# Two layers of graph attention on one core: bracket's middle formed on VectorE, unit matrix of R added by GpSimd

## Chip, cores and metric
One core of a Trainium2 chip runs the whole program. The metric is the device time in microseconds (us). Engines: TensorE (PE; its weight loads are PEld), VectorE (DVE), ScalarE (ACT), GpSimd (POOL) and SyncE (SP), which issues the DMAs.

## What is computed
Layer 0 is a four-head graph attention over 4096 nodes; layer 1 is the one that the change touches. Cut to what matters:

```python
def top_p(Xa):                          # A: 4096 x 4096, row by row
    probs = softmax((Xa @ W1.T @ W2.T) @ (Xa @ W3.T).T)
    # keep the largest entries of a row until their sum reaches 0.9, drop the rest
    A = probs * mask
    return A / A.sum(-1)

R = adj + eye(N)                        # unit matrix on top of the adjacency
R = R / R.sum(-1)
Z = 0; Xf = Xa = X
for n in range(2):
    A = top_p(Xa)
    Xf = R @ Xf
    Xa = A @ Xa
    Z = Z + Xf @ U1[n].T + Xa @ U2[n].T
h = X + Z                               # then a layer norm, X added, a second layer norm
```

## The kernel before
Rows are handled in 32 tiles of 128. Layer 0 fills the first 1.6 ms. Layer 1 runs in two steps, `s` = 0 and 1. Step 1 (from 2.43 ms on) is where all of the change lies. Its engines each run their own program through the iterations n = 0, 1, ... of one software pipeline, and meet at semaphores only, so the order of an engine's instructions is that in which the code issues them:

- **TensorE** (`Tr`, `logits`, `zx`, `AV`, `mq`, `Rmul`): turns the masked row tile n-1, multiplies the logits of tile n+1, forms A @ Xa for tile n-1, a small product for tile n-2, and two row tiles of R @ Xf. The matrix R is never formed: `Rstart` (L690 to L697) puts the product of the identity with the tile's own rows of Xf into the PSUM bank, and `Rpart` adds 32 products with the adjacency's blocks, 257 columns wide; the last column of Xf is 1, so it collects the row sum of R.
- **ScalarE** (`expo`, `level`, `av_ev`, `mq_ev`, `r_ev`): softmax's exponential for tile n+1 (L971, then three small ones for the row's eight largest, `e8`), and for the same tile three levels of the top-p search (`level`, L979 to L1002). A level is two passes over 4096 columns (L988, L989) and five small operations that move the threshold; the first level starts with L987, which waits on semaphore `bt`, and its L995 waits on `bf`. `av_ev` (L1010) copies A @ Xa out of PSUM, `mq_ev` (L949, L952) two smaller results, `r_ev` (L1018) a row tile of R @ Xf.
- **VectorE** (`search`, `threshold`, `finish`): from ScalarE's threshold for tile n (semaphore `lt`, L1222) it makes levels 4 and 5 (L1226, each one pass over 4096 columns with two inputs from SBUF), then `rmax(n+1)` (L1173, L1174: the eight largest logits of the next tile, which lets ScalarE start `expo(n+1)`), then level 6 (L1226), `final_stats`, the pass L1232, and sixteen maxima, a sort of 48 candidates and some twenty small operations. It signals `lv`, marks entries (L1293, L1294), waits for GpSimd's all-reduce (L1334) and writes the masked tile (L1345).
- **GpSimd** (`r_post`, `bracket`, `scale_a`, `accumulate`, `final_second`, `final_first`, `levels`, `final_add`), in this order in an iteration: `r_post` scales two row tiles of R @ Xf by the reciprocal of their row sums; `bracket(n+1)` (L463 to L488) waits on `e8` and computes where the search starts: the middle `tst` = square root of (a6 * a4), signalled as `bt` after L475, then the factors of all levels, signalled as `bf` after L486; `scale_a` (L492 to L498) waits for `av_ev`, `accumulate` (L506) for `mq_ev`; `levels` (L460) is a maximum over partitions (`partition_all_reduce`).

Which iterations have the last layer norms is set by `fslot`: for n from 17 on, `final_add`, `final_first` and `final_second` (L525 to L541) stand on GpSimd between `accumulate` and `levels`, and four rows of `final_stats` (L1193 to L1196) on VectorE ahead of L1232. So the cycles up to 3536 us (called early ones here) and those from 3593 us (late ones) carry different work.

```python
b = rslot()
mm(b[:, 0:XA], ident_s, xf[:, r % NT, :], start=True, stop=False)      # L696
...
plink(tt(a(8), a(6), a(4), ALU.mult))                                   # L474
tt(tst[:, t % 2:t % 2 + 1], a(8), ahalf, ALU.pow).then_inc(g["bt"], 1)  # L475
```

`plink`, `link` and `alink` make the engine wait until its own instruction has finished. The functions that the change touches:

Of the kernel before, what the change touches and what calls it, by code (L numbers as in the profile page):

```python
# [9 lines left out]
ALU = mybir.AluOpType  # L10
# [5 lines left out]
TOP_P = 0.9  # L16
# [5 lines left out]
GEO = (0, 6)  # L22
ACT_LEVELS = 3
BISECT = 42


def gat_topp_kernel(nc, xT, x, adj, adjTb, Wp, WT, aT, res_w, bias, res_b, ident, sel,
                    W1, W2T, W3T, U1T, U2T, ln_g, ln_b, out):
    N = adj.shape[0]
    NT = N // 128  # L30
# [12 lines left out]
    AJR = 4  # L43
# [17 lines left out]
    with ctx:  # L61
# [208 lines left out]
        for s in range(2):  # L270
            g = {}
            for n in ("kt", "kc", "km", "kk", "pl", "el", "mx", "xp", "mask", "av", "R", "rv", "pz", "gx",
                      "gd", "po", "rd", "xs", "acc", "nz", "hi", "gi", "yd", "ys", "fi", "fa", "s1", "f1", "s2",
                      "fo", "fd", "lv", "lr", "lt", "qd", "e8", "bt", "bf", "xc"):
                g[n] = sem(f"{n}_{s}")
            g["aj"] = [sem(f"aj{i}_{s}") for i in range(AJR)]
            g["xd"] = [sem(f"xd{i}_{s}") for i in range(2)]
            st.append(g)
# [149 lines left out]
        def _(po):  # L428
# [26 lines left out]
            for s in range(2):  # L455
# [6 lines left out]
                def bracket(t):  # L462
                    a = lambda i: ptm[:, i:i + 1]  # L463
                    Z = zE[:, t % 2:t % 2 + 1]
                    po.wait_ge(g["e8"], t + 1)
                    h7, g7 = e8[:, 7:8], am[:, 8:9]
                    ts(a(0), Z, TOP_P, None, ALU.mult)
                    ts(a(1), h7, -1.0, 1.0, ALU.mult, ALU.add)  # L468
                    plink(ts(a(2), Z, (1 - TOP_P) / 4096 / 1.0001, None, ALU.mult))
                    ts(a(3), g7, a(0), None, ALU.is_ge)  # L470
                    plink(tt(a(5), h7, a(2), ALU.subtract))
                    ts(a(4), a(1), a(3), h7, ALU.mult, ALU.add)
                    plink(ts(a(6), a(5), a(3), a(2), ALU.mult, ALU.add))
                    plink(tt(a(8), a(6), a(4), ALU.mult))  # L474
                    tt(tst[:, t % 2:t % 2 + 1], a(8), ahalf, ALU.pow).then_inc(g["bt"], 1)  # L475
                    plink(tt(a(7), a(6), mone, ALU.pow))
                    plink(tt(a(9), a(7), a(4), ALU.mult))
                    f = fac[:, t % 2]
                    f2 = f.rearrange("p a b -> p (a b)")
                    plink(ts(f2, ones[:, 0:2 * LV], a(9), None, ALU.mult))  # L480
                    plink(tt(f2, f2, exps.rearrange("p a b -> p (a b)"), ALU.pow))
                    plink(ts(f[:, :, LV - 1], f[:, :, LV - 1], 1.0 + 2.0 ** -12, None, ALU.mult))
                    w = avg[:, t % 2]
                    tt(w[:, 0, :], f[:, 0, :], f[:, 1, :], ALU.add)
                    plink(tt(w[:, 1, :], f[:, 1, :], f[:, 0, :], ALU.subtract))
                    plink(ts(havg[:, t % 2].rearrange("p a b -> p (a b)"), w.rearrange("p a b -> p (a b)"),  # L486
                             0.5, None, ALU.mult))
                    po.sem_inc(g["bf"], 1)  # L488
# [19 lines left out]
                def r_post(p):  # L508
                    for i in range(2):
                        r = 2 * p + i  # L510
                        po.wait_ge(g["rd"], r + 1)
                        plink(tt(pq[:, 1, i:i + 1], prs[:, i, 256:257], mone, ALU.pow))
                        if p >= 1:
                            po.wait_ge(g["ys"], 32 * p)
                        o = ts(yr[:, i, :], prs[:, i, 0:256], pq[:, 1, i:i + 1], 0.0, ALU.mult, ALU.add)
                        if r < NT:
                            plink(o)
                            po.wait_ge(g["gi"], 32 * (p + 1))
                            o = tt(yr[:, i, :], yr[:, i, :], gxi[:, i, :], ALU.add)
                        o.then_inc(g["yd"], 1)  # L520
# [52 lines left out]
        def _(pe):  # L573
# [98 lines left out]
            for s in range(2):  # L672
# [17 lines left out]
                    return bank(6 + i % 2)  # L690

                def Rstart(r):
                    b = rslot()
                    if r >= NT:
                        pe.wait_ge(s_xl[r % NT // CT], 48)
                    mm(b[:, 0:XA], ident_s, xf[:, r % NT, :], start=True, stop=False)  # L696
                    return b  # L697

                def Rpart(r, b, lo, hi):
                    for j in range(lo, hi):  # L700
                        c, e = divmod(j, TBK)
                        q = r * NCH + c
                        if e == 0:
                            pe.wait_ge(g["aj"][q % AJR], 16 * (q // AJR + 1))
                        if r >= NT and j % CT == 0:
                            pe.wait_ge(s_xl[j // CT], 48)
                        last = mm(b[:, 0:XA], aj[:, q % AJR, e, :], xf[:, j, :], start=False, stop=(j == NT - 1))  # L707
                        if e == TBK - 1:
                            last.then_inc(g["R"], 1)

# [126 lines left out]
        def _(ac):  # L837
# [66 lines left out]
            for s in range(2):  # L904
# [119 lines left out]
                for t in range(2):  # L1024
                    zx_ev(None, t)
                    mq_ev(None, t)
                    if s == 0:
                        gx_ev(t)
                def acts(t, items):
                    items = list(items)  # L1030
                    for k in range(1, ACT_LEVELS + 1):
                        if t < NT:
                            level(t, k)
                        if k >= ACT_LEVELS - 1 and items:
                            r_ev(items.pop(0))
                    for r in items:
                        r_ev(r)
# [5 lines left out]
                for n in range(NT + 2):  # L1043
# [13 lines left out]
                        zx_ev(tz, tx)  # L1057
                    if n + 1 < NT:
                        expo(n + 1)
                    if 1 <= n <= NT:  # L1060
                        av_ev(n - 1)
                    if zm:
                        mq_ev(tz, tx)
                    if s == 0 and tx is not None:
                        gx_ev(tx)
                    if s == 1:
                        acts(n + 1, [2 * p + i for p in pairs_in(n) for i in range(2)])
                barrier(ac, kS[s])

        @block.vector  # L1070
        def _(ve):
# [94 lines left out]
            for s in range(2):  # L1166
# [32 lines left out]
                def final_stats(n):  # L1199
# [4 lines left out]
                    if s == 1 and n - 1 in fslot:  # L1204
                        for r in (2 * fslot[n - 1], 2 * fslot[n - 1] + 1):
                            ve.wait_ge(g["fa"], r + 1)
                            stats_of(r, g["s1"])

                def search(t):
                    E = eb[:, t % 2, 0:N]  # L1210
                    VN = V[:, 0:N]
# [2 lines left out]
                    if r:  # L1214
                        ve.wait_ge(g["xp"], t + 1)
                        link(v.tensor_scalar(theta, Z, TOP_P, None, ALU.mult))
                        if t == 0:
                            ve.wait_ge(g["bf"], 1)
                            link(v.tensor_copy(mid, tst[:, 0:1]))
                        else:  # L1220
# [2 lines left out]
                        for k in range(ACT_LEVELS + 1 if t else 1, r + 1):  # L1223
                            if k == r and t + 1 < NT:
# [3 lines left out]
                            link(v.tensor_scalar(tmp, G, theta, avg[:, t % 2, 1, k - 1:k], ALU.is_lt, ALU.mult))  # L1228
                            link(v.scalar_tensor_tensor(out=mid, in0=tmp, scalar=fac[:, t % 2, 0, k - 1:k], in1=mid,
                                                        op0=ALU.add, op1=ALU.mult))  # L1230
                        final_stats(t)
                        link(v.scalar_tensor_tensor(out=VN, in0=E, scalar=mid, in1=E, op0=ALU.is_le,  # L1232
                                                    op1=ALU.mult, accum_out=G))
                        link(v.tensor_tensor(ghi, Z, G, ALU.subtract))
# [176 lines left out]
```

## Time and profile before
| | |
|---|---|
| Median of 3 runs | 4351.58 us (4349.74 to 4353.28) |
| Profiled execution: its time | 4350.77 us |
| Profiled execution: span from the first instruction to the last | 4349.0 us |
| PE busy | 3762.5 us, 87% |
| DVE busy | 3623.6 us, 83% |
| ACT busy | 3114.5 us, 72% |
| POOL busy | 1017.3 us, 23% |
| Mean granted TensorE clock | 0.942 |

The busy shares are means over the whole program. No engine is near 100%, so within a stage the order in which engines wait for each other counts: the chain of waits follows the work that ended last back from one instruction to what released it, and the timeline shows what each engine did meanwhile. Times in both count from the start of the span.

### The profile page before, as it was taken

The page shows a single profiled execution, that of the slowest core. Times are in us where ns is not written, and L with a number is a line of the kernel's source. Part 1 is how long each engine was busy: PE and PEld are TensorE (multiplying, and loading weights), DVE is VectorE, ACT ScalarE, POOL GpSimd, SP SyncE. Part 2 cuts the span into 40 slices and gives each one's busy share as a digit, 9 for nine tenths or more (in the row PEclk, how much of TensorE's full clock was granted, in tenths as well). Part 3 has the DMA queues.
Part 4 walks back from the last instruction along what each step waited for, and adds up shares of the span by engine and source line. Part 5 has one row for each costly group of instructions (what it writes and reads, how often), then busy time and mean ns, then how long its engine had stood idle before and what let it go on. Part 6 is the DMA issues. An engine that isn't in the chain of part 4 may idle for free.

```text
span 4349.0 us, 66313 instructions
## 1 busy us (share of the span) xinstructions
PE 3762.5 (87%) x25364; PEld 3163.1 (73%) x25364; DVE 3623.6 (83%) x6400; ACT 3114.5 (72%) x3128; POOL 1017.3 (23%) x1412
## 2 busy tenths in 40 slices
PE   8677877777777769999999749999999999999996
PEld 5677777777777747777778547777777777778875
DVE  2899999999999939888888188888888889999995
ACT  3789889898989845555555367777777777777771
POOL 0000000000000000001010224444444445555555
PEclk9899999999999989999999979999999999999998
DMA  3211111111111020000000212222233423333332
GB/s 116 93 45 66 45 55 56 47 64 47 64 47 64 27 78 12 19 16 19 16 17 17 87 35 85 87 83 88 88 93 93 134 90 105 107 107 105 100 104 73
DMA packets 131759, 292.49 MB, mean 67 GB/s; under 512 B 14122, under 2 KB 94186, under 8 KB 127058
## 3 DMA queue, kind: packets, MB, share of 16 engines
q1 hardware_dynamic: 131410, 287.99, 20.6%
q8 instruction: 201, 3.29, 0.3%
q14 instruction: 148, 1.21, 0.1%
HBM read 250.19 MB, written 37.75 MB: 66 GB/s over the span
## 4 chain that ended last, share of the span: by engine, by line
PE 34%; ACT 28%; DVE 14%; issue 14%; POOL 10%; DMA 1%; DVEq 0%; SPq 0%; ACTq 0%; POOLq 0%
PE ps L803 11%; PE ps L642 9%; DVE b L1226 7%; ACT b L871 6%; ACT b L988 5%; ACT b L989 5%; DVE b L1173 3%; ACT b L865 3%; PE ps L792 3%; ACT b L971 3%; PE ps L748 3%; PE ps L623 2%; POOL b L468 2%; ACT b L859 1%; PE ps L780 1%
## 5 line engine op out<-in xcount | busy, mean ns | idle before, releaser
L707 PE MATMUL ps<-b 128*128 128x257 f32 x4096 | 902.1, 379 | 0.0
L803 PE MATMUL ps<-b 128*128 128x257 f32 x4096 | 900.9, 379 | 0.0
L642 PE MATMUL ps<-cb,b 128*128 128x128 f32 x4096 | 606.9, 312 | 321.7 <-ACT b L865 321.7
L707 PEld LDWEIGHTS ps<-b 128*128 128x128 f32 x4096 | 775.6, 189 | 118.3 <-issue 3.8
L803 PEld LDWEIGHTS ps<-b 128*128 128x128 f32 x4096 | 770.2, 189 | 111.7
L642 PEld LDWEIGHTS ps<-cb,b 128*128 128x128 f32 x4096 | 546.1, 163 | 371.1 <-ACT b L865 329.6
L1137 DVE SCALAR_TENSOR_TENSOR b<-b 128x4096 f32<-128x4096 f32 x128 | 566.4, 4425 | 63.1 <-ACT b L859 59.8
L1139 DVE CUSTOM_DVE_ANT_0 b<-b 128x4096 f32<-128x4096 f32 x128 | 566.3, 4425 | 5.5 <-DMA b<-in_adj 1.1
L871 ACT ACTIVATE b<-ps 128x1024 f32<-128x1024 f32 x512 | 499.9, 1023 | 75.6 <-PE ps L642 74.0
L623 PE MATMUL ps<-b 128*64 128x128 f32 x8192 | 504.0, 276 | 0.0
L865 ACT ACTIVATE b<-b 128x4096 f32<-128x4096 f32 x128 | 474.4, 3706 | 8.0 <-DVE b L1141 8.0
L623 PEld LDWEIGHTS ps<-b 128*64 128x64 f32 x8192 | 442.5, 137 | 43.1 <-issue 39.7
L1226 DVE SCALAR_TENSOR_TENSOR b<-b 128x4096 f32<-128x4096 f32 x99 | 453.0, 4576 | 2.6 <-DVE b L1222 0.2
L792 PE MATMUL ps<-cb,b 128*128 128x128 f32 x2048 | 265.5, 291 | 172.4 <-DVE b L1345 115.0
L792 PEld LDWEIGHTS ps<-cb,b 128*128 128x128 f32 x2048 | 250.6, 151 | 201.0 <-DVE b L1345 121.7
L436 POOL TENSOR_TENSOR cb<-cb 128x1 f32<-128x1 f32 x32 | 39.4, 1231 | 1518.6 <-DVE cb L1123 1518.6
L971 ACT ACTIVATE b<-b 128x4096 f32<-128x4096 f32 x64 | 237.0, 3704 | 197.9 <-DVE b L1174 197.9
L988 ACT ACTIVATE b<-b 128x4096 bf16<-128x4096 f32 x93 | 345.0, 3709 | 7.7 <-ACT b L1018 5.7
L989 ACT ACTIVATE b<-b 128x4096 bf16<-128x4096 f32 x93 | 345.0, 3709 | 3.0
L1345 DVE SCALAR_TENSOR_TENSOR b<-b 128x4096 f32<-128x4096 f32 x64 | 287.0, 4484 | 67.2 <-issue 41.7
L859 ACT ACTIVATE b<-b 128x2560 f32<-128x2560 f32 x128 | 310.9, 2430 | 2.3 <-SPq L216 2.3
L1051 ACT ACTIVATE b<-ps 128x1024 f32<-128x1024 f32 x256 | 244.5, 1029 | 59.8 <-PE ps L792 55.2
(186 smaller groups left out, 4743.2 us busy)
## 6 DMA issues: line engine op xcount, KB each, us to landing
b<-in_adjTb SPq DMA_DIRECT2D x256, 512.0 KB, 3.8
b<-in_adj SPq DMA_DIRECT2D x32, 2048.0 KB, 8.0
y_d<-b SPq DMA_DIRECT2D x64, 128.0 KB, 1.7
h_d<-b SPq DMA_DIRECT2D x64, 128.0 KB, 1.8
b<-h_d SPq DMA_DIRECT2D x64, 128.0 KB, 2.3
b<-in_xT SPq DMA_DIRECT2D x1, 4096.0 KB, 15.8
b<-in_x SPq DMA_DIRECT2D x32, 128.0 KB, 2.2
b<-y_d SPq DMA_DIRECT2D x32, 128.0 KB, 2.1
```

The source lines that it names most:

```text
L623: last = mm(bank(6 + t % 2)[half, 128 * h:128 * h + 128], h_s[:, j, 64 * h:64 * h + 64], pt[:, gq % PTR, b, :], start=(j < 2), stop=(j >= ...
L642: last = nc.tensor.transpose(bank(2 * (gq % 3), 2)[:, b * 128:(b + 1) * 128], ub[:, u % UB, j * 128:(j + 1) * 128], ident_s)
L707: last = mm(b[:, 0:XA], aj[:, q % AJR, e, :], xf[:, j, :], start=False, stop=(j == NT - 1))
L792: last = nc.tensor.transpose(o[:, b * 128:(b + 1) * 128], eb[:, t % 2, j * 128:(j + 1) * 128], ident_s)
L803: last = mm(o[:, 0:XA], at[:, q % ATR, b, :], xa[:, j, :], start=(j == 0), stop=(j == NT - 1))
L865: act(b, b, ACT.Exp, bias=nm[:, u:u + 1], accum_out=zp[:, u:u + 1]).then_inc(s_x, 1)
L871: act(pt[:, gq % PTR].rearrange("p a b -> p (a b)"), bank(2 * (gq % 3), 2)[:, 0:CW], ACT.Copy).then_inc(s_ev, 1)
L988: alink(act(junk, e, ACT.Sign, bias=neg, accum_out=C))
L989: alink(act(junk, e, ACT.Relu, bias=neg, accum_out=S))
L1137: link(v.scalar_tensor_tensor(out=b, in0=b, scalar=SLOPE, in1=b, op0=ALU.mult, op1=ALU.max))
L1139: link(v.tensor_tensor_reduce(out=b, in0=b, in1=adj_s[:, t % 2, :], scale=1.0, scalar=-3.0e38, op0=ALU.mult, op1=ALU.max, accum_out=nm[:, ...
L1226: link(v.scalar_tensor_tensor(out=VN, in0=E, scalar=mid, in1=E, op0=ALU.is_gt, op1=ALU.mult, accum_out=G))
```

## The change
Three things are changed, all in step 1.

1. **The bracket's middle.** VectorE forms the product under the root in three small operations (`bracket_head`), between its level 6 and `final_stats`, and signals `bh`. GpSimd's `bracket` waits for that instead of `e8` and takes the root as its first operation; the product a8 is gone, the rest of `bracket` follows. VectorE's pass over the tile (L1232 before, L1249 now) waits for the root (`bt`).
2. **ScalarE's order.** `av_ev` and `mq_ev` stood between `expo` and the first level. In step 1 they now stand behind the first level.
3. **The unit matrix of R.** `Rstart` issues no product any more, the first adjacency block starts the sum, and `r_post` on GpSimd adds the tile's rows of Xf (257 columns, the ones among them) ahead of the reciprocal.

```diff
--- before.py
+++ after.py
@@ -22,6 +22,7 @@
 GEO = (0, 6)
 ACT_LEVELS = 3
 BISECT = 42
+LEAST = (1 - TOP_P) / 4096 / 1.0001
 
 
 def gat_topp_kernel(nc, xT, x, adj, adjTb, Wp, WT, aT, res_w, bias, res_b, ident, sel,
@@ -271,7 +272,7 @@
             g = {}
             for n in ("kt", "kc", "km", "kk", "pl", "el", "mx", "xp", "mask", "av", "R", "rv", "pz", "gx",
                       "gd", "po", "rd", "xs", "acc", "nz", "hi", "gi", "yd", "ys", "fi", "fa", "s1", "f1", "s2",
-                      "fo", "fd", "lv", "lr", "lt", "qd", "e8", "bt", "bf", "xc"):
+                      "fo", "fd", "lv", "lr", "lt", "qd", "e8", "bt", "bf", "xc", "bh"):
                 g[n] = sem(f"{n}_{s}")
             g["aj"] = [sem(f"aj{i}_{s}") for i in range(AJR)]
             g["xd"] = [sem(f"xd{i}_{s}") for i in range(2)]
@@ -462,17 +463,17 @@
                 def bracket(t):
                     a = lambda i: ptm[:, i:i + 1]
                     Z = zE[:, t % 2:t % 2 + 1]
-                    po.wait_ge(g["e8"], t + 1)
+                    po.wait_ge(g["bh"], t + 1)
+                    m = tst[:, t % 2:t % 2 + 1]
+                    tt(m, m, ahalf, ALU.pow).then_inc(g["bt"], 1)
                     h7, g7 = e8[:, 7:8], am[:, 8:9]
                     ts(a(0), Z, TOP_P, None, ALU.mult)
                     ts(a(1), h7, -1.0, 1.0, ALU.mult, ALU.add)
-                    plink(ts(a(2), Z, (1 - TOP_P) / 4096 / 1.0001, None, ALU.mult))
+                    plink(ts(a(2), Z, LEAST, None, ALU.mult))
                     ts(a(3), g7, a(0), None, ALU.is_ge)
                     plink(tt(a(5), h7, a(2), ALU.subtract))
                     ts(a(4), a(1), a(3), h7, ALU.mult, ALU.add)
                     plink(ts(a(6), a(5), a(3), a(2), ALU.mult, ALU.add))
-                    plink(tt(a(8), a(6), a(4), ALU.mult))
-                    tt(tst[:, t % 2:t % 2 + 1], a(8), ahalf, ALU.pow).then_inc(g["bt"], 1)
                     plink(tt(a(7), a(6), mone, ALU.pow))
                     plink(tt(a(9), a(7), a(4), ALU.mult))
                     f = fac[:, t % 2]
@@ -509,6 +510,7 @@
                     for i in range(2):
                         r = 2 * p + i
                         po.wait_ge(g["rd"], r + 1)
+                        plink(tt(prs[:, i, :], prs[:, i, :], xf[:, r % NT, :], ALU.add))
                         plink(tt(pq[:, 1, i:i + 1], prs[:, i, 256:257], mone, ALU.pow))
                         if p >= 1:
                             po.wait_ge(g["ys"], 32 * p)
@@ -690,11 +692,7 @@
                     return bank(6 + i % 2)
 
                 def Rstart(r):
-                    b = rslot()
-                    if r >= NT:
-                        pe.wait_ge(s_xl[r % NT // CT], 48)
-                    mm(b[:, 0:XA], ident_s, xf[:, r % NT, :], start=True, stop=False)
-                    return b
+                    return rslot()
 
                 def Rpart(r, b, lo, hi):
                     for j in range(lo, hi):
@@ -704,7 +702,7 @@
                             pe.wait_ge(g["aj"][q % AJR], 16 * (q // AJR + 1))
                         if r >= NT and j % CT == 0:
                             pe.wait_ge(s_xl[j // CT], 48)
-                        last = mm(b[:, 0:XA], aj[:, q % AJR, e, :], xf[:, j, :], start=False, stop=(j == NT - 1))
+                        last = mm(b[:, 0:XA], aj[:, q % AJR, e, :], xf[:, j, :], start=(j == 0), stop=(j == NT - 1))
                         if e == TBK - 1:
                             last.then_inc(g["R"], 1)
 
@@ -1026,11 +1024,16 @@
                     mq_ev(None, t)
                     if s == 0:
                         gx_ev(t)
-                def acts(t, items):
+                def acts(t, items, n):
                     items = list(items)
                     for k in range(1, ACT_LEVELS + 1):
                         if t < NT:
                             level(t, k)
+                        if k == 1:
+                            if 1 <= n <= NT:
+                                av_ev(n - 1)
+                            if n >= 2 or n + 2 < NT:
+                                mq_ev(n - 2 if n >= 2 else None, n + 2 if n + 2 < NT else None)
                         if k >= ACT_LEVELS - 1 and items:
                             r_ev(items.pop(0))
                     for r in items:
@@ -1057,14 +1060,15 @@
                         zx_ev(tz, tx)
                     if n + 1 < NT:
                         expo(n + 1)
-                    if 1 <= n <= NT:
-                        av_ev(n - 1)
-                    if zm:
-                        mq_ev(tz, tx)
-                    if s == 0 and tx is not None:
-                        gx_ev(tx)
-                    if s == 1:
-                        acts(n + 1, [2 * p + i for p in pairs_in(n) for i in range(2)])
+                    if s == 0:
+                        if 1 <= n <= NT:
+                            av_ev(n - 1)
+                        if zm:
+                            mq_ev(tz, tx)
+                        if tx is not None:
+                            gx_ev(tx)
+                    else:
+                        acts(n + 1, [2 * p + i for p in pairs_in(n) for i in range(2)], n)
                 barrier(ac, kS[s])
 
         @block.vector
@@ -1206,6 +1210,14 @@
                             ve.wait_ge(g["fa"], r + 1)
                             stats_of(r, g["s1"])
 
+                def bracket_head(t):
+                    Z = zE[:, t % 2:t % 2 + 1]
+                    ve.wait_ge(g["e8"], t + 1)
+                    link(v.scalar_tensor_tensor(out=x_, in0=Z, scalar=TOP_P, in1=am[:, 8:9], op0=ALU.mult,
+                                                op1=ALU.is_le))
+                    link(v.scalar_tensor_tensor(out=x_, in0=Z, scalar=LEAST, in1=x_, op0=ALU.mult, op1=ALU.max))
+                    v.tensor_scalar(tst[:, t % 2:t % 2 + 1], x_, e8[:, 7:8], None, ALU.mult).then_inc(g["bh"], 1)
+
                 def search(t):
                     E = eb[:, t % 2, 0:N]
                     VN = V[:, 0:N]
@@ -1215,6 +1227,7 @@
                         ve.wait_ge(g["xp"], t + 1)
                         link(v.tensor_scalar(theta, Z, TOP_P, None, ALU.mult))
                         if t == 0:
+                            bracket_head(0)
                             ve.wait_ge(g["bf"], 1)
                             link(v.tensor_copy(mid, tst[:, 0:1]))
                         else:
@@ -1228,7 +1241,11 @@
                             link(v.tensor_scalar(tmp, G, theta, avg[:, t % 2, 1, k - 1:k], ALU.is_lt, ALU.mult))
                             link(v.scalar_tensor_tensor(out=mid, in0=tmp, scalar=fac[:, t % 2, 0, k - 1:k], in1=mid,
                                                         op0=ALU.add, op1=ALU.mult))
+                        if t + 1 < NT:
+                            bracket_head(t + 1)
                         final_stats(t)
+                        if t + 1 < NT:
+                            ve.wait_ge(g["bt"], t + 2)
                         link(v.scalar_tensor_tensor(out=VN, in0=E, scalar=mid, in1=E, op0=ALU.is_le,
                                                     op1=ALU.mult, accum_out=G))
                         link(v.tensor_tensor(ghi, Z, G, ALU.subtract))
```

The lines of the changed file stand two or more lower or higher than those of the kernel before; the instructions below say which is which. A row gives line, operation, output and inputs (b is the pool of SBUF, ps is PSUM, cb the constants), its width, and the semaphores it waits for.

GpSimd, a late iteration, from the second row tile of `r_post` on, before:

```order
L512 TENSOR_TENSOR b<-b,cb 128x1 [waits rd_1]
L515 TENSOR_SCALAR b<-b 128x256 [waits ys_1,s_pc]
L467 TENSOR_SCALAR b<-b 128x1 [waits e8_1]
L468 TENSOR_SCALAR b<-b 128x1
L469 TENSOR_SCALAR b<-b 128x1
L470 TENSOR_SCALAR b<-b 128x1 [waits s_pc]
L471 TENSOR_TENSOR b<-b 128x1
L472 TENSOR_SCALAR b<-b 128x1 [waits s_pc]
L473 TENSOR_SCALAR b<-b 128x1
L474 TENSOR_TENSOR b<-b 128x1 [waits s_pc]
L475 TENSOR_TENSOR b<-b,cb 128x1 [waits s_pc]
L476 TENSOR_TENSOR b<-b,cb 128x1
```

and now:

```order
L513 TENSOR_TENSOR b<-b 128x257 [waits rd_1]
L514 TENSOR_TENSOR b<-b,cb 128x1 [waits s_pc]
L517 TENSOR_SCALAR b<-b 128x256 [waits ys_1,s_pc]
L468 TENSOR_TENSOR b<-b,cb 128x1 [waits bh_1]
L470 TENSOR_SCALAR b<-b 128x1
L471 TENSOR_SCALAR b<-b 128x1
L472 TENSOR_SCALAR b<-b 128x1
L473 TENSOR_SCALAR b<-b 128x1 [waits s_pc]
L474 TENSOR_TENSOR b<-b 128x1
L475 TENSOR_SCALAR b<-b 128x1 [waits s_pc]
L476 TENSOR_SCALAR b<-b 128x1
L477 TENSOR_TENSOR b<-b,cb 128x1 [waits s_pc]
```

The root (L475 before, L468 now) has moved from the ninth place of `bracket` to the first; the product L474 is gone; each row tile of `r_post` has one instruction more, L513.

VectorE, a late iteration, from `rmax`'s last instruction on, as it is now:

```order
L1178 TENSOR_SCALAR b<-b 128x1 [waits s_dv]
L1239 SCALAR_TENSOR_TENSOR b<-b 128x4096
L1241 TENSOR_SCALAR b<-b 128x1 [waits s_dv]
L1242 SCALAR_TENSOR_TENSOR b<-b 128x1 [waits s_dv]
L1216 SCALAR_TENSOR_TENSOR b<-b 128x1 [waits e8_1,s_dv]
L1218 SCALAR_TENSOR_TENSOR b<-b 128x1 [waits s_dv]
L1219 TENSOR_SCALAR b<-b 128x1 [waits s_dv]
L1197 BN_STATS b<-b 128x6 [waits f1_1]
```

The three instructions L1216, L1218 and L1219 are new; L1197 is the first of `final_stats`, and at the end of `final_stats` stands the pass that now waits for `bt_1` as well:

```order
L1199 TENSOR_SCALAR b<-b 128x1 [waits s_dv]
L1200 TENSOR_SCALAR b<-b 128x1
L1249 SCALAR_TENSOR_TENSOR b<-b 128x4096 [waits s_dv,bt_1]
L1251 TENSOR_TENSOR b<-b 128x1 [waits s_dv]
L1255 MAX b<-b 128x8 [waits s_dv]
L1255 MAX b<-b 128x8 x15
```

ScalarE, the first of the three levels and what stands around it, before:

```order
L1010 ACTIVATE b<-ps 128x257 [waits s_ac,xs_1,av_1]
L949 ACTIVATE b<-ps 128x256 [waits s_ac,acc_1,pl_1]
L952 ACTIVATE kr<-ps 128x128 [waits s_ac]
L987 ACTIVATE b<-b 128x1 [waits s_ac,bt_1]
L988 ACTIVATE b<-b 128x4096 [waits s_ac]
L989 ACTIVATE b<-b 128x4096 [waits s_ac]
L990 ACTIVATE b<-b 128x1 [waits s_ac]
L991 ACTIVATE b<-b 128x1 [waits s_ac]
L992 ACTIVATE b<-b 128x1 [waits s_ac]
L995 ACTIVATE b<-b 128x1 [waits bf_1,s_ac]
L997 ACTIVATE b<-b 128x1 [waits s_ac]
```

and now:

```order
L985 ACTIVATE b<-b 128x1 [waits s_ac,bt_1]
L986 ACTIVATE b<-b 128x4096 [waits s_ac]
L987 ACTIVATE b<-b 128x4096 [waits s_ac]
L988 ACTIVATE b<-b 128x1 [waits s_ac]
L989 ACTIVATE b<-b 128x1 [waits s_ac]
L990 ACTIVATE b<-b 128x1 [waits s_ac]
L993 ACTIVATE b<-b 128x1 [waits bf_1,s_ac]
L995 ACTIVATE b<-b 128x1 [waits s_ac]
L1008 ACTIVATE b<-ps 128x257 [waits xs_1,av_1,s_ac]
L947 ACTIVATE b<-ps 128x256 [waits s_ac,acc_1,pl_1]
L950 ACTIVATE kr<-ps 128x128 [waits s_ac]
L986 ACTIVATE b<-b 128x4096 [waits s_ac]
```

L1010, L949 and L952 (now L1008, L947 and L950) have moved behind L997 (now L995).

## Rows read from the trace of the kernel before
**Rows 1.** Source view of line L1174 (VectorE), 2518 to 3537 and 3592 to 4209 us.
```profile
L1174 DVE TENSOR_SCALAR b<-b x19: 153/154/155, 2518.6 to 3536.3; 128x1 f32<-128x1 f32 x19
L1174 DVE TENSOR_SCALAR b<-b x12: 153/154/155, 3593.1 to 4208.0; 128x1 f32<-128x1 f32 x12
```

**Rows 2.** Chain of waits, 3196 to 3239 us: start us, us, what.
```profile
3196.69 0.16 DVE b L1174
...
3201.75 0.26 POOL b L467
3202.07 4.31 POOL b L468
...
3207.95 0.20 POOL b L474
3208.23 0.58 POOL b L475
3208.83 0.21 ACT b L987
...
3238.23 0.16 DVE b L1222
```

**Rows 3.** Timeline, same cycle: start us, us, engine, line, operation, shapes.
```profile
3201.84 4.48 DVE L1232 SCALAR_TENSOR_TENSOR b<-b 128x4096 f32<-128x4096 f32 x1
...
3213.31 0.25 POOL L486 TENSOR_SCALAR b<-b 128x12 f32<-128x12 f32 x1
...
3204.08 0.39 ACT L1010 ACTIVATE b<-ps 128x257 f32<-128x257 f32 x1 [2.47 <-PE ps L803]
...
3217.81 0.39 ACT L995 ACTIVATE b<-b 128x1 f32<-128x1 f32 x1
```

**Rows 4.** Chain of waits, 3759 to 3815 us, one later cycle.
```profile
3759.60 0.17 DVE b L1174
...
3774.48 0.23 POOL b L492
...
3786.63 0.73 POOL b L541
...
3793.14 0.40 POOL b L460
...
3799.25 0.17 DVE b L1222
...
3814.56 0.16 DVE b L1174
```

**Rows 5.** Timeline of VectorE and GpSimd, same later cycle.
```profile
3764.50 0.22 DVE L1229 SCALAR_TENSOR_TENSOR b<-b 128x1 f32<-128x1 f32 x1
3764.76 0.43 DVE L1193 BATCH_NORM_STATS2 b<-b 128x6 f32<-128x256 f32 x1
...
3768.91 4.49 DVE L1232 SCALAR_TENSOR_TENSOR b<-b 128x4096 f32<-128x4096 f32 x1
...
3768.90 2.31 POOL L481 TENSOR_TENSOR b<-b 128x12 f32<-128x12 f32 x1
3771.30 2.19 POOL L482 TENSOR_SCALAR b<-b 128x2 f32<-128x2 f32 x1
```

**Rows 6.** Timeline of VectorE and GpSimd in the cycle at 3870 us.
```profile
3878.94 4.49 DVE L1232 SCALAR_TENSOR_TENSOR b<-b 128x4096 f32<-128x4096 f32 x1
...
3879.14 6.45 POOL L481 TENSOR_TENSOR b<-b 128x12 f32<-128x12 f32 x1
...
3886.91 0.23 POOL L492 TENSOR_SCALAR b<-b 128x1 f32<-128x1 f32 x1 [0.19 <-POOL b L486]
```

**Rows 7.** Waits of TensorE, 2520 to 3536 and 3593 to 4208 us: total, times, longest.
```profile
PE ps L792 <- ACT b L1051: 57.0, 18, 4.7
PE ps L792 <- DVE b L1345: 35.1, 11, 4.4
```

**Rows 8.** Groups of instructions: the product with the identity.
```profile
L696 PE MATMUL ps<-b,cb 128*128 128x257 f32 x128 | 38.9, 386 | 3.7 <-SPq L216 3.7
```

## The prediction
> **What bounds the kernel now.** The page comes first: no engine is near 100%, so the sum is not to be made from busy times. All edits lie in step 1, and there one instruction per row tile marks the cycle: L1174, with which VectorE releases ScalarE's exponential. The source view gives its first and last start [rows 1]: 18 early cycles from 2518.6 to 3536.3 us, 56.54 us each, and 11 late ones from 3593.1 to 4208.0, 55.9 each. The chain of waits then says what closes a cycle; below, times count from L1174's start.
>
> An early cycle [rows 2]: exponential and e8 until 5.06, where GpSimd's bracket begins; its root is out and ScalarE's L987 starts at 12.14; three levels; VectorE takes over at 41.54 (L1222) and the rest of the cycle, 15.0, goes to levels 4 and 5 and `rmax`. VectorE, idle before L1222, and TensorE, which waits in every cycle for ScalarE's copies (57.0 us in 18 waits [rows 7]), are not the bound. The striking row is L468: 4.31 us for one column. It started just after L1232 (at 5.15, 4.48 us long [rows 3]) and came out when that pass ended.
>
> A late cycle closes elsewhere [rows 4]: not the levels on ScalarE but GpSimd's queue. scale_a starts at 14.88, the layer norms end at 27.76, the all-reduce starts at 33.54 (5.8 us in which the page shows nothing, since GpSimd changes its configuration for it), then VectorE writes the tile and reaches L1222 at 39.65. Here whatever makes GpSimd late makes the cycle late.
>
> **The change, early cycles.** Before, L1229 of level 6 is followed by L1193 0.26 us later [rows 5]; in the early cycles level 6 ends at 5.15, where L1232 starts [rows 3]. Three linked operations at 0.27 each: the third starts at 5.70 and ends near 5.9. GpSimd needs about a tenth to start, 0.58 for the root (L475 [rows 2]): ScalarE starts at 6.6, not 12.14. Gross gain 5.5.
>
> Two things take it back. First, the rest of bracket. VectorE's pass waits for the root, so it starts at 6.6 too, not 5.15, and again one of GpSimd's next operations gets stuck behind it. L468 came free 4.54 after the pass's start [rows 2, 3], and from there to the end of L486 it was 7.18 [rows 2, 3]; without the product (0.28, L474 to L475) and the root (0.58) 6.32 remain. The factors come at 6.6 + 4.54 + 6.32 = 17.5, 0.6 later than before (16.87). ScalarE's L995 reads them 8.98 after L987's start [rows 2, 3], so it would be there at 15.6; with 0.14 for the signal it gets them at 17.65, a new wait of 2.1. Second, the PSUM copies: they lay in the wait for the root and cost nothing (L1010 at 7.39, 0.39 long [rows 3]); that cover is gone, and three instructions of 0.4 or less with the gaps between them are 1.5 on the path (1.1 if there were no gaps, 2 if each ended a wait of its own). From L995 to L1222 it was 20.42 [rows 2, 3], now 21.9: L1222 at 39.6, and with 15.0 a cycle of 54.6. Saved: 2.0 x 18 = 35 us.
>
> **Late cycles.** VectorE's third operation is out at 5.9, the four row statistics take 4.15 (3764.76 to 3768.91 [rows 5]), so the pass starts at 9.97, not 9.31. The root is long there, no wait. On GpSimd L481, which raises the factors to their powers, starts at 9.30 today [rows 5], 4.24 after bracket's first operation; without product and root that is 3.38, behind the new root, which ends at 6.56: 9.94. So again it starts just ahead of the pass, as now (3768.90 against 3768.91 [rows 5]), runs its 2.31 beside it, and the next one (L482) is stuck until the pass ends. The factors came at 14.7, just ahead of L492, and come at 15.35, in time for ScalarE at 15.6. But scale_a, which waited only for bracket to end (14.88), now waits for av_ev, behind the first level: 6.6 + 8.98 to L995, 0.7 for it and L997, 0.4 for the copy, 0.15 for the signal = 16.85. **GpSimd's whole queue moves 1.97 us later,** the all-reduce and L1222 with it, since VectorE waits for that all-reduce in each late cycle. ScalarE's own levels would be done at 6.6 + 29.4 [rows 2] + 1.5 = 37.5, so what they gain ends in a wait. Twelve such cycles (the last one, from 4208.0 on, too) cost 23.6.
>
> One late cycle is already disturbed: at 3870 us L481 started 0.20 after the pass and took 6.45 [rows 6]. ScalarE's e8 had come late there; now VectorE waits for e8 as well, so both shift alike and some 2.4 come back. Late cycles net: +21.
>
> **Edits with one answer.** The cycle at 3536 us, with two of the four statistics, loses what it gains within 0.3. The first bracket, for which VectorE has nothing else to do, gets 0.5 longer. The products with the identity take at most 38.9 us in all [rows 8], on an engine that waits anyway [rows 7]: 0. The bound below is a gain of that size. The two additions on GpSimd per iteration, 257 columns, are priced by L541 at 0.73 [rows 4]. In the worst case they push the bracket by 1.5 a cycle, 45 us in all; but between the second row tile and the next bracket GpSimd has nothing to do: 0. In an early cycle the all-reduce starts 2 us later, VectorE's wait for it has that much room because its pass is 1.5 later too: 0.
>
> Sum against the profiled execution: 4350.8 - 35 + 21 + 1 = **4338 us**. The median shown, 4351.6, stands 0.8 above; I leave the forecast at 4338.
>
> **A rule against the trace.** L481 runs beside the whole first half of L1232, and that pass keeps its 4.49 [rows 5]. The Trainium skill, page "SBUF — State Buffer", section "Who interferes with whom", says that a VectorE instruction with two SBUF inputs contends with a GpSimd one that reads SBUF, and that whichever issued first has the shared ports for its whole instruction. The second half of that does not hold for this power operation; that the later one is fully blocked agrees with L468's 4.31 and L481's 6.45. By the row the sum stays at 4338; by the rule L481, starting clearly ahead, would hold the pass back, and the time would be the last rival's 4365.
>
> **Rivals.**
> - **L481 loses its race (20%, slower).** The 0.03 us by which it leads is less than I can know; the deciding point is L481 starting after L1249, VectorE's pass. For the lead: the first operation of bracket today carries a start-up that its successor need not have. Against: both ends of the sum are uncertain by 0.1. The price is shown [rows 6]: L492 followed 7.97 after the pass's start. So the factors come near 17.8, ScalarE waits for them, ends the level and av_ev at 19.05, and scale_a starts at 19.2, 4.3 later than now. 12 x 4.3 less the 2.4 of the cycle that already has it is 49: 4350.8 - 35 + 1 + 49 = 4366 us.
> - **Some late cycles lose it (13%).** With half of them, 4352: no change.
> - **The late cycles do not get longer (7%).** If the all-reduce's start does not follow the queue (the 5.8 us ahead of it are not broken down by any row), the 21 us fall away: 4317.
> - **TensorE counts after all (3%).** Were its 64 products worth their time, up to 39 us more would go, 4300 to 4320. Against it stand its waits [rows 7].
> - **GpSimd holds the pass (5%, slower).** If L481, now ahead, keeps VectorE from its pass for 2.3, the operation behind it gets stuck until the pass ends at 16.8; factors at 17.7, ScalarE waits 2.1, and the price is that of the first rival within 2 us: 4365.
>
> **How the numbers follow.** The forecast has 52%, with a spread of 8 us for the signals and for the copies' 1.5 (0.2 wrong there is 6 us over 30 cycles). A measurement of this kernel can tell about 0.2% from no change, 8.7 us. Faster by more than that means below 4342.9: most of the forecast (42), the 7 and the 3, 52%. Within: the rest of the forecast and most of the mixed case, 23%. Slower: the two slow rivals, 25%. The range 4320 to 4371 holds the forecast, the mixed and both slow cases; it leaves out about half of the 10% at the fast end.
>
> **What would show it.** Right: L468 (the root now) at 6.0 and ScalarE's L985 at 6.6 after L1178; a wait of L993 for GpSimd's L487 of about 2 us in early cycles and none in late ones; early cycles of 54.6, late ones near 57.8 with scale_a (L493) at 16.9; L482 at 2.31 in late cycles, L483 at over 2. Wrong: L482 at 6 us in late cycles (first rival); early cycles above 55.5, or a TensorE that no longer waits in them; late cycles at 56.

## The result, and the profile after
| | before | changed |
|---|---|---|
| Median of 8 runs each | 4350.86 us | 4364.65 us |
| Ratio, 95% interval | | 1.0031 (1.0021 to 1.0042) |
| Profiled execution, span | 4349.0 us | 4363.4 us |
| Mean granted TensorE clock | 0.942 | 0.936 |
| 18 early cycles, each | 56.54 us | 54.73 us |
| 11 late cycles, each | 55.9 us | 59.7 us |

The forecast was 4338 us, 13 below the kernel before; the kernel became slower by 14 us. The first rival had 4366. A cycle is counted as in the prediction, from the start of VectorE's L1178 to the next one. The source view of L1178, the former L1174 [rows 1], has the first and last start of the early and of the late cycles:

```profile
L1178 DVE TENSOR_SCALAR b<-b x19: 153/154/156, 2518.6 to 3503.7; 128x1 f32<-128x1 f32 x19
L1178 DVE TENSOR_SCALAR b<-b x12: 153/154/155, 3560.0 to 4216.8; 128x1 f32<-128x1 f32 x12
```

Early cycles gave 18 x 1.8 = 33 us back (35 forecast). The 11 late ones cost 42, the last one, up to the end of the span, 5.6 more, and the cycle between them gained 0.6: 42 + 5.6 - 33 - 0.6 = 14. On the mean of the 11 late cycles scale_a starts at 19.0 instead of 15.1 (+3.9; 15.1 is 14.9 in ten cycles and 17.3 in the disturbed one), the stretch from the end of the layer norms to the all-reduce is 0.3 shorter, and the one from VectorE's takeover (L1235, the former L1222) to the next L1178 is 0.2 longer: +3.8.

A late cycle of the changed kernel, chain of waits, start us, us, what (it answers to [rows 4]):

```profile
3738.88 0.15 DVE b L1178
...
3744.42 0.22 DVE b L1219
...
3744.72 0.55 POOL b L468
...
3745.36 0.26 POOL b L470
...
3748.81 6.57 POOL b L482
...
3756.65 0.40 ACT b L993
...
3757.91 0.23 POOL b L493
...
3770.03 0.74 POOL b L543
...
3776.94 0.40 POOL b L461
...
3783.36 0.16 DVE b L1235
...
3798.67 0.15 DVE b L1178
```

Times from here on count from the start of L1178. GpSimd's root (L468) is out at 6.4, near the 6.6 of the forecast. The powers (L482) take 6.57, so the factors reach ScalarE's L993 at 17.8, after which it ends its level and makes the copies; scale_a (L493) starts at 19.0, not at 14.9; the layer norms end at 31.9, the all-reduce starts at 38.1, and VectorE takes over at 44.5. Why the powers take that long is in the timeline of VectorE, to be read beside [rows 5] (start us, us, line):

```profile
3744.03 0.16 DVE L1216 SCALAR_TENSOR_TENSOR b<-b 128x1 f32<-128x1 f32 x1
3744.22 0.16 DVE L1218 SCALAR_TENSOR_TENSOR b<-b 128x1 f32<-128x1 f32 x1
3744.42 0.21 DVE L1219 TENSOR_SCALAR b<-b 128x1 f32<-128x1 f32 x1
3744.55 0.42 DVE L1197 BATCH_NORM_STATS2 b<-b 128x6 f32<-128x256 f32 x1
...
3748.71 4.49 DVE L1249 SCALAR_TENSOR_TENSOR b<-b 128x4096 f32<-128x4096 f32 x1 [0.16 <-DVE b L1200]
```

The pass L1249 starts at 3748.71, the powers 0.10 behind it at 3748.81, and they last until 2.2 after the pass has ended. In all 11 late cycles it is the same (min/median/max in ns):

```profile
L482 POOL TENSOR_TENSOR b<-b x11: 6557/6560/6563, 3569.9 to 4167.1; 128x12 f32<-128x12 f32 x11
```

VectorE's total wait for the all-reduce in these cycles, before and now (total, times, longest):

```profile
DVE b L1334 <- POOL b L460: 20.2, 11, 3.0
```

```profile
DVE b L1351 <- POOL b L461: 58.2, 11, 5.5
```

An early cycle, chain of waits of the changed kernel, beside [rows 2]. The operation behind the root (L470) is stuck for 4.54, ScalarE waits for the factors (L993), and the copies L1008 to L950 stand in the chain. VectorE takes over with L1235 and then makes its passes L1239:

```profile
3235.49 0.55 POOL b L468
...
3236.13 4.54 POOL b L470
...
3247.45 0.40 ACT b L993
...
3248.20 0.40 ACT b L1008
...
3249.34 0.29 ACT kr L950
...
3269.68 4.50 DVE b L1239 x2
```

```profile
ACT b L993 <- POOLq L489: 43.6, 18, 2.4
```

43.6 us in 18 cycles is a wait of 2.4 in each; 2.1 was forecast.

### The profile page after: what moved, and what is told of

It reads as the page before. It is cut to its first block, busy times and chain, and to the rows that moved or that the text cites. A ratio compares the mean times of both kernels' runs of the same rounds, so it can differ in the third digit from the quotient of the medians.

```text
span 4363.4 us, 66204 instructions
## 1 busy us (share of the span) xinstructions
PE 3742.9 (86%) x25236; PEld 3151.4 (72%) x25236; DVE 3640.0 (83%) x6496; ACT 3115.4 (71%) x3128; POOL 1094.0 (25%) x1444
## 4 chain that ended last, share of the span: by engine, by line
PE 34%; ACT 22%; DVE 16%; issue 15%; POOL 12%; DMA 1%; DVEq 0%; SPq 0%; ACTq 0%; POOLq 0%
PE ps L801 11%; PE ps L644 9%; DVE b L1239 9%; ACT b L869 7%; PE ps L790 4%; DVE b L1177 3%; ACT b L863 3%; ACT b L987 3%; ACT b L986 3%; POOL b L482 3%; PE ps L746 3%; PE ps L625 2%; POOL b L470 2%; ACT b L857 1%; PE ps L778 1%
## 5 line engine op out<-in xcount | busy, mean ns | idle before, releaser
L644 PE MATMUL ps<-cb,b 128*128 128x128 f32 x4096 | 606.0, 312 | 322.3 <-ACT b L863 322.3
L644 PEld LDWEIGHTS ps<-cb,b 128*128 128x128 f32 x4096 | 546.0, 163 | 371.8 <-ACT b L863 329.7
L869 ACT ACTIVATE b<-ps 128x1024 f32<-128x1024 f32 x512 | 499.7, 1023 | 73.8 <-PE ps L644 72.6
L790 PE MATMUL ps<-cb,b 128*128 128x128 f32 x2048 | 281.1, 302 | 203.8 <-DVE b L1362 162.1
L1239 DVE SCALAR_TENSOR_TENSOR b<-b 128x4096 f32<-128x4096 f32 x99 | 451.2, 4557 | 2.4
L790 PEld LDWEIGHTS ps<-cb,b 128*128 128x128 f32 x2048 | 265.7, 158 | 233.2 <-DVE b L1362 170.8
```

What stands on the lines that cost most here:

```text
L644: last = nc.tensor.transpose(bank(2 * (gq % 3), 2)[:, b * 128:(b + 1) * 128], ub[:, u % UB, j * 128:(j + 1) * 128], ident_s)
L790: last = nc.tensor.transpose(o[:, b * 128:(b + 1) * 128], eb[:, t % 2, j * 128:(j + 1) * 128], ident_s)
L869: act(pt[:, gq % PTR].rearrange("p a b -> p (a b)"), bank(2 * (gq % 3), 2)[:, 0:CW], ACT.Copy).then_inc(s_ev, 1)
```

## Experiments
Theory A says: a late cycle lasts as long as GpSimd's queue up to the all-reduce; that queue grew because the powers lost their race with VectorE's pass by 0.1 us, and because scale_a now waits for copies that stand behind the first level. The rivals put it on the additions in GpSimd's queue (B), on TensorE (C), or want one of the two causes alone (D, F). All times are medians; each ratio is to runs of the kernel before taken with it.

**e1, the unit matrix as before.**

```diff
-                    return rslot()
+                    b = rslot()
...
+                    mm(b[:, 0:XA], ident_s, xf[:, r % NT, :], start=True, stop=False)
+                    return b
...
-                        plink(tt(prs[:, i, :], prs[:, i, :], xf[:, r % NT, :], ALU.add))
...
```

> The changed kernel with the product with the identity put back and the addition on GpSimd taken out (bracket and the order on ScalarE as changed). Theory A (the race of GpSimd's powers with VectorE's pass, and scale_a behind the first level, make the late cycles long): the unit matrix has no part in it, 4365 us within 2, late cycles 59.7 us as in the changed kernel. Rival B (GpSimd's two additions per iteration, 1.3 to 1.5 us, lengthen the queue that bounds the late cycles): 4365 - 12 x 1.4 = 4348. Rival C (TensorE's time counts, the products gave back up to 28 us): up to 4392.

Measured: 4370.85 us, ratio 1.0053 (1.0040 to 1.0067). Taking the additions out did not help, so B is out. The median is 6 us above the changed kernel's, where A had allowed 2; the two intervals (1.0040 to 1.0067, 1.0021 to 1.0042) just meet, but each of the five runs of e1 is above all eight of the changed kernel, so a small difference is likely. The source view of its L1181:

```profile
L1181 DVE TENSOR_SCALAR b<-b x19: 153/154/155, 2517.5 to 3503.5; 128x1 f32<-128x1 f32 x19
L1181 DVE TENSOR_SCALAR b<-b x12: 153/154/155, 3560.7 to 4224.2; 128x1 f32<-128x1 f32 x12
```

GpSimd's wait ahead of the all-reduce in the late cycles, in e1 and then in the changed kernel (total, times, longest):

```profile
POOL b L461 <- issue: 72.7, 11, 6.8
```

```profile
POOL b L461 <- issue: 66.2, 11, 6.2
```

The early cycles are those of the changed kernel within 0.05 us, the late ones 0.6 longer, and as much is added to the time between the end of the layer norms and the all-reduce: 72.7 against 66.2 us in 11 cycles. What sets it is open. C, up to 28 us on TensorE, is not what was measured; e4 tests it again.

**e2, VectorE's pass later.** Work is added, in order to lose less:

```diff
                         if t + 1 < NT:
+                            link(v.tensor_copy(y_, x_))
                             ve.wait_ge(g["bt"], t + 2)
```

> The changed kernel with one copy of a single column more on VectorE, after the row statistics and ahead of the pass that waits for the root; it makes the pass start about 0.2 us later in the late cycles. Theory A: GpSimd's powers then start 0.1 ahead of the pass instead of 0.1 behind it, take 2.3 us instead of 6.6, scale_a starts at 16.6 instead of 19.0, late cycles shrink by 2.4 to 57.3: 4365 - 12 x 2.4 = 4336 us, from added work. Rival B (the additions on GpSimd): 4365 to 4367, since nothing of the queue changes. Rival C: the same as B.

Measured: 4338.98 us, 0.9975 (0.9966 to 0.9984). One copy of 0.2 us makes the changed kernel 26 us faster. That it lands where the forecast stood is in part luck: early cycles gave 38 us instead of 35, late ones took 58.0 instead of 57.8. The powers now take 2.3 us in every late cycle, while the pass keeps its length (cycle mark, powers, pass):

```profile
L1178 DVE TENSOR_SCALAR b<-b x12: 153/154/155, 3553.6 to 4191.6; 128x1 f32<-128x1 f32 x12
...
L482 POOL TENSOR_TENSOR b<-b x11: 2313/2314/2317, 3563.5 to 4142.3; 128x12 f32<-128x12 f32 x11
...
L1250 DVE SCALAR_TENSOR_TENSOR b<-b x11: 4484/4485/4486, 3563.6 to 4142.4; 128x4096 f32<-128x4096 f32 x11
```

The late cycles took 58.0, not the 57.3 expected: scale_a starts at 16.8 (16.6), and the stretch between the layer norms and the all-reduce is 71.0 us in 11 cycles instead of 66.2. Most of what is missing there came in the early ones, 54.4 instead of 54.7, which the expectation had left alone: the pass starts 0.08 later there too, and the first operation behind the root, which had started 0.05 after it, now starts 0.03 ahead and is not stopped. The same race, with a smaller prize; L470 in early cycles, in the changed kernel and in e2:

```profile
L470 POOL TENSOR_SCALAR b<-b x17: 4527/4533/4535, 2578.1 to 3455.2; 128x1 f32<-128x1 f32 x17
```

```profile
L470 POOL TENSOR_SCALAR b<-b x17: 259/259/270, 2576.6 to 3447.8; 128x1 f32<-128x1 f32 x17
```

**e3, the copies back ahead of the first level.**

```diff
                     items = list(items)
+                    if 1 <= n <= NT:
+                        av_ev(n - 1)
+                    if n >= 2 or n + 2 < NT:
+                        mq_ev(n - 2 if n >= 2 else None, n + 2 if n + 2 < NT else None)
...
-                        if k == 1:
-                            if 1 <= n <= NT:
...
```

> The changed kernel with av_ev and mq_ev back between the exponential and the first level. Theory A: scale_a waits only for bracket again, 17.8 instead of 19.0 in late cycles (12 x 1.2 = 15 us); in early cycles the copies end at 9.5, ScalarE's first level starts at 9.7 instead of 6.4, but no longer waits 2.4 us for the factors and has no copies behind it, so the levels end at 38.9 instead of 39.7 (18 x 0.8 = 14 us): 4365 - 29 = 4336 us. Rival D (moving the copies behind the first level is what makes the change save anything in early cycles): early cycles get longer than 54.7 us, over 55.5, and the time is 4365 or more.

Measured: 4336.92 us, 0.9969 (0.9957 to 0.9981). Both kinds of cycle got shorter, so D falls: the move of the copies was not what gained time in early cycles, it cost time there as well. The hit on 4337 is luck in its parts: early cycles took 53.5 (53.9 expected), late ones 59.2 (58.5 expected). scale_a came at 17.8 as expected, but the stretch ahead of the all-reduce was 74.4 us in 11 cycles instead of 66.2.

```profile
L1177 DVE TENSOR_SCALAR b<-b x19: 153/154/155, 2519.0 to 3482.8; 128x1 f32<-128x1 f32 x19
L1177 DVE TENSOR_SCALAR b<-b x12: 153/154/156, 3539.1 to 4190.6; 128x1 f32<-128x1 f32 x12
```

**e4, the third edit alone** on the kernel before (no product, the addition in `r_post`).

> The kernel before with the third edit alone: no product with the identity, the rows of Xf added on GpSimd. Theory A: neither TensorE nor that part of GpSimd's queue is waited for, 4351 us within 2. Rival B: + 12 x 1.4 or more, 4368. Rival C: faster by up to 28 us, 4323.

Measured: 4348.33 us, 0.9997 (0.9988 to 1.0006). No difference, with early cycles of 56.4 and late ones of 56.1 (56.5 and 55.9 before): on the kernel before neither side of that edit is waited for. The granted clock of 0.937, close to the changed kernel's 0.936, came without a change of time.

**e5, the copies inside the first level.** They are called in `level`, for k = 1, one line ahead of `ac.wait_ge(g["bf"], t + 1)`, and no longer behind it.

> The changed kernel with av_ev and mq_ev put inside the first level, just ahead of its wait for the factors. Theory A: in early cycles the 1.5 us of copies fill the 2.4 us wait, the levels end at 38.1 instead of 39.7, cycle 53.1; in late cycles the copies are done before GpSimd's bracket, scale_a waits for bracket alone, 17.8 instead of 19.0, cycle 58.5: 4365 - 18 x 1.6 - 12 x 1.2 = 4322 us. Rival E (TensorE becomes the bound as soon as early cycles fall under some 53.5 us): early cycles of 54, 4337 as with the copies ahead of the level.

Measured: 4329.28 us, 0.9948 (0.9935 to 0.9962). Early cycles took 53.1, so E, TensorE as the bound below some 53.5, is out at that length; late ones took 59.05, 0.5 more than expected, again between the layer norms and the all-reduce (73.8 us in 11 cycles).

**e6, e5 and e2 together.**

> The last one and the extra copy on VectorE that lets GpSimd's powers start first. Theory A: early cycles 52.9, late ones 12 x (2.2 + 1.2) less than in the changed kernel, 56.3: 4365 - 18 x 1.8 - 12 x 3.4 = 4292 us, below the kernel before. Rival E: early cycles of 54, 4312.

Measured: 4294.48 us, 0.9866 (0.9851 to 0.9881): faster than both kernels, 59 us below the median of the kernel before taken with it (4353.34).

```profile
L1182 DVE TENSOR_SCALAR b<-b x19: 153/154/155, 2521.3 to 3473.2; 128x1 f32<-128x1 f32 x19
L1182 DVE TENSOR_SCALAR b<-b x12: 153/154/155, 3529.7 to 4150.6; 128x1 f32<-128x1 f32 x12
...
L482 POOL TENSOR_TENSOR b<-b x11: 2313/2314/2317, 3539.7 to 4104.1; 128x12 f32<-128x12 f32 x11
```

**e7, the race lost in the kernel before.** The test from the other side:

```diff
+                    plink(ts(a(10), a(6), 1.0, None, ALU.mult))
                     plink(tt(a(7), a(6), mone, ALU.pow))
```

> The kernel before with one linked operation of a single column more on GpSimd, between the root and the reciprocal in bracket; it delays the powers by 0.3 us and nothing that ScalarE waits for. Theory A: in the late cycles the powers start 0.3 behind VectorE's pass instead of 0.01 ahead, take 6.2 instead of 2.3, and everything behind them on GpSimd is 2.3 later; early cycles do not change: 4351 + 11 x 2.2 = 4375 us. Rival F (a lost race is not enough, only the move of the copies lengthens late cycles): 4351 + 12 x 0.3 = 4354.

Measured: 4375.97 us, 1.0057 (1.0043 to 1.0070). An operation of 0.3 us, for which ScalarE does not wait, costs 23 us. The early cycles stay as they were. In 10 of the 11 late ones the powers start 0.35 behind the pass and take 6.3 us; in the eleventh the operation ahead of them (L481) is stopped for 4.54 instead. In the last cycle, from 4233.5 on, they start at 4243.18, the pass at 4243.19, and they take 2.31:

```profile
L1175 DVE TENSOR_SCALAR b<-b x19: 153/154/155, 2518.2 to 3536.7; 128x1 f32<-128x1 f32 x19
L1175 DVE TENSOR_SCALAR b<-b x12: 153/154/155, 3593.6 to 4233.5; 128x1 f32<-128x1 f32 x12
...
L482 POOL TENSOR_TENSOR b<-b x11: 2310/6304/6310, 3603.3 to 4185.5; 128x12 f32<-128x12 f32 x11
```

**e8, the second edit alone** on the kernel before (the copies behind the first level).

> The kernel before with the second edit alone, the copies behind the first level. Theory A: early cycles lose the cover of the copies and gain nothing, + 1.5; in late cycles ScalarE starts its level at 8.0, scale_a comes at 18.3 instead of 14.9, + 3.4: 4351 + 18 x 1.5 + 12 x 3.4 = 4419 us. Rival F: + 12 x 3.4 is all or more, 4392 or beyond 4430. Rival G (the all-reduce absorbs it): 4378.

Measured: 4429.99 us, 1.0178 (1.0164 to 1.0191), 11 us over the expectation. The powers keep their 2.3 us here, and late cycles still go from 55.9 to 59.9: the move alone is enough. scale_a comes at 18.3 as expected; 0.65 of the 4.0 are again in the stretch ahead of the all-reduce (76.3 us in 11 cycles, 69.1 before), and the cycle at 3564 us, which the expectation had not counted, took 61.3 instead of 56.9. Rival G (the all-reduce absorbs the delay, 4378) is out. Early cycles, at 58.2, pay 1.6 us for the copies:

```profile
L1180 DVE TENSOR_SCALAR b<-b x19: 153/153/155, 2516.7 to 3563.8; 128x1 f32<-128x1 f32 x19
L1180 DVE TENSOR_SCALAR b<-b x12: 153/154/155, 3625.1 to 4283.6; 128x1 f32<-128x1 f32 x12
...
L481 POOL TENSOR_TENSOR b<-b x11: 2308/2308/2309, 3634.4 to 4233.2; 128x12 f32<-128x12 f32 x11
```

With e7 this settles F: each cause lengthens the late cycles by itself. They do not add up, since scale_a waits for whichever is later: of its 3.9 us in the changed kernel, taking back the race gives 2.2 (e2), taking back the move 1.2 (e3).

**e9, e3 and e2 together.**

> The copies ahead of the first level (as in e3) and one copy more on VectorE ahead of the pass (as in e2). Theory A: the two effects add up in late cycles, where GpSimd's powers start first and scale_a waits for bracket alone, 12 x 2.2 less than e3: 4337 - 27 = 4310 us. If the late cycles had another floor than GpSimd's queue (VectorE's own work, TensorE), it would be 4325 or more.

Measured: 4294.52 us, 0.9866 (0.9850 to 0.9883), 15 us less than expected and the same as e6. Late cycles took 56.3, so they have no other floor above that. Half of the 15 us lies in the stretch ahead of the all-reduce, 66.5 us in 11 cycles against 74.4 in e3, the other half in early cycles of 53.1 instead of 53.5, by the early race of e2.

**e10, e6 with three copies ahead of the pass.**

> The kernel of e6 with three single-column copies on VectorE ahead of the pass instead of one, so that GpSimd's powers (2.31 us) start some 0.5 us ahead of it. Theory A (whoever starts second is stopped, but the powers read their input at once and then hold nothing): the pass starts 0.4 later, keeps its 4.49 us, late cycles within 0.5 of e6, 4294 to 4300. Rule of the Trainium skill (SBUF page: the first has the ports for its whole instruction): the pass starts or ends 1.8 us later still, the operation behind the powers is stuck until then, bracket's factors come at 17 instead of 15.4 and late cycles are up to 1.7 longer: 4315.

Measured: 4295.07 us, 0.9863 (0.9847 to 0.9880). Timelines of GpSimd and VectorE in one late cycle:

```profile
3761.76 2.32 POOL L482 TENSOR_TENSOR b<-b 128x12 f32<-128x12 f32 x1
3764.17 2.63 POOL L483 TENSOR_SCALAR b<-b 128x2 f32<-128x2 f32 x1
```

```profile
3761.65 0.15 DVE L1252 COPY b<-b 128x1 f32<-128x1 f32 x1
3761.84 0.15 DVE L1253 COPY b<-b 128x1 f32<-128x1 f32 x1
3762.03 0.15 DVE L1254 COPY b<-b 128x1 f32<-128x1 f32 x1
3762.22 4.49 DVE L1256 SCALAR_TENSOR_TENSOR b<-b 128x4096 f32<-128x4096 f32 x1
```

The powers start 0.46 us ahead of the pass and run 1.86 into it; the pass starts right behind the third copy and takes 4.49 as ever. Only the next operation, L483, is stopped. Late cycles took 56.7 (56.4 in e6), and the time is in the 4294 to 4300 of A, not at the 4315 of the rule.

## Why the prediction was wrong
**Early cycles: right.** The sum said 54.6, measured were 54.73, and the steps are those of the sum (measured in brackets): root out at 6.6 (6.4), a new wait of ScalarE of 2.1 (2.4), the copies on the path. One operation is stuck as forecast, but the 6.32 of the sum count from the second operation of bracket, and it was the first one. e3 adds what the sum had not weighed: the copies could have stayed where they were.

**Late cycles: the mechanism was right, its branch was wrong.** GpSimd's queue bounds them, and they lengthen with scale_a; e7 and e8 show that. VectorE's wait for the all-reduce, up from 20.2 to 58.2 us, is where the gain of the levels went. The step that failed is "So again it starts just ahead of the pass, as now", 9.94 against 9.97. Measured were 9.93 for the powers and 9.83 for the pass, so the order was the reverse.

The mis-sized term is GpSimd's stretch from the start of VectorE's third small operation to the powers: 4.24 in the sum (5.70 to 9.94), 4.39 measured. 0.09 of that is the gap between the root's end (3745.27) and the next operation (3745.36), which the sum had put at 0. Another 0.07 is in the rest of bracket, 3.45 and not 3.38. Most of it comes from taking the root out with its length of 0.58, although on the kernel before the next operation starts 0.53 after it (L475 at 3767.02, L476 at 3767.55). VectorE's stretch was right, 4.27 in the sum and 4.29 measured, although its working does not come out as written: a third operation out at 5.9 and 4.15 for the statistics make 10.05, not 9.97. The three small operations had been priced at 0.27 each. The two whose successor waits for them took 0.19 and 0.20, which moved both engines' starts forward alike and decided nothing.

So 0.15 us turned the +1.97 of a late cycle into +3.8, and e2, which turns the order back with 0.2 us, takes the late cycles to 58.0, near the 57.8 of the forecast.

**The chance.** The text called the lead less than it could know, and still gave the branch 52 against 20. Its one argument for the lead, a start-up of bracket's first operation that a successor need not have, did not hold: behind the root that operation took the same 0.26, with the gap of 0.09 on top. The rows gave two ends 0.03 apart, each uncertain by 0.1, and no reason to prefer one order. The measured time lies in the range of 4320 to 4371 only because the range takes in the slow rivals.

**The first rival** was right in its price: 4366, powers stopped in every late cycle, scale_a at 19.2 (19.0). Part of the 2 us of agreement is luck: late cycles cost 3.8 each and not 4.3, the last one 5.6.

**The unit matrix and the identity:** 0 on the kernel before (e4), as in the sum. Within the changed kernel taking it back cost 6 us (e1). The sum had no term for that, and its cause, in the stretch ahead of the all-reduce, stays open.

**The rule on the ports.** The Trainium skill, page "SBUF — State Buffer", section "Who interferes with whom", was right on the later one being stopped (powers of 6.56 us in 11 of 11 late cycles). That the first keeps the ports for its whole instruction did not hold for the powers: with a lead of 0.1 (e2) and 0.46 (e10) the pass started on time and kept its 4.49. So the prediction's last rival, in which GpSimd holds the pass, is out.

## What to carry to other kernels
Where an operation of one engine stops one of another, and the two start within a few tenths of each other, the order of the two starts is the quantity to predict, with its error, and if it cannot be had the two outcomes deserve like chances; a tiny operation on either side then decides it on purpose. Before an operation is moved behind a long one, ask who waits for its result: here GpSimd's queue, which closed the late cycles, 12 of 31, waited for a copy of 0.4 us. The copies were best placed inside a wait that ScalarE had anyway (e5), or ahead of the level (e3); with the race won, the two places gave the same time (e6, e9).

## What the hardware showed beyond the question
The interval between GpSimd's last ordinary operation and its all-reduce is not constant. In it the trace has no operation of GpSimd, only two changes of the engine's configuration at its start. Its mean over the 11 late cycles was 6.0 us in e6, e9, e10 and the changed kernel, 6.2 to 6.5 in the kernel before, e2, e4 and e7, 6.6 in e1, 6.7 to 6.8 in e3 and e5, and 6.9 in e8. Single cycles of one kernel differ by up to 1.5 us (5.9 to 7.3 in e2), but the means are far enough apart to move a kernel's time by 6 to 8 us. The interval does not follow the time at which it begins: e1 and the changed kernel begin it within 0.1 us of each other. No run was made to find its cause.
